# A decoder layer on one core: every engine's order rewritten without a loop, value products in one run, maxima transposed 128 columns wide, the context laid out transposed

## The chip, the core and the metric

The kernel runs on 1 of the 8 cores of a Trainium2 chip. A core has five engines, each with its own queue of instructions that it takes strictly in order: TensorE (PE, matrix products and transposes, with weight loads shown apart as PEld), VectorE (DVE), ScalarE (ACT), GpSimd (POOL) and SyncE (SP), which here issues all the transfers (DMAs). They are tied by semaphores alone. The metric is device time in microseconds (us), lower is better.

## What is computed

The reference is one decoder layer in float32 on 32 batches of 128 tokens by 128 features, with 16 heads of 8: self-attention with a bias by relative position, cross-attention on a context with a padding mask, and a feed-forward part whose activations are rounded to 8 bits and whose weights are ternary.

```
x = x + attn(LN(LN(x)))                  # softmax(q k / sqrt(8) + bias(i - j)) v, then w_out
x = x + xattn(LN(x), ctx, ctx, mask)     # the same with keys and values of ctx, masked scores
x = x + ffn(LN(x))                       # silu(gate) * up, then down; act_quant before each product
```

## The kernel before

All 32 batches stay in SBUF (`x_all`). Each batch goes through three stages, S (self-attention), X (cross-attention) and F (feed-forward), and one step of the program works on about nine batches at once, each at another place of the layer: `step(st)` of each engine calls its functions with `st.seq(lag)`, the batch that is `lag` steps behind. Lags are the table `FRONT_S, A_S, B_S, FRONT_X, A_X, B_X, POST_X, FFN2 = 0, 2, 3, 4, 5, 6, 7, 8`. Steps 0 to 9 and 30 to 39 are written out, steps 10 to 29 are five turns of a loop with four steps in it, in which semaphore values are worked out in registers.

What happens to one batch in an attention stage `a` (S or X):

- `normalise` (DVE) makes `xn`; TensorE transposes it (L1175, L1196), ACT copies it to `xnT`; `project_s` and `project_x` (L1210, L1224, L1225) give queries and keys, L1214 and L1192 the values, which ACT copies into `v_aug`.
- Queries and keys are split into three bf16 parts: `part1`, `part2` on ACT, `rest`, `part3` on POOL. SP writes them to HBM (`parts_out`, scratch, L288) and reads them back in another layout (`stack_in`, one transfer to `stack_q`, L306, and three to `stack_k`, L311).
- `scores_a` (L1059, four chunks `c` of four heads, banks 0 and 1) gives scores whose negated row maxima DVE takes (`row_max`, L826). POOL splits them into two bf16 parts of 16 columns (`neg_max_parts`, 32 columns), TensorE transposes them (`max_transposed`, L1154), ACT copies them (`maxT_out`), SP puts them into two rows of the stack (`max_in`, L327).
- `scores_b` (L1092, banks 2 and 3) gives the transposed scores less the maximum, ACT takes `exp` (L533) into `probs`, which S and X share, and `attend` (L1117, 4 products of 32 output rows each in a quarter of the array, for each of 4 chunks) multiplies with `v_aug`. In X a matrix product of 128x512 puts the mask into the bank first (L1055, L1088).
- `o_raw_out` (ACT), `o_transposed` (PE), `attend_sums` and `attend_norm` (DVE), `on_transposed`, `oT_out`, `project_out` (L1264), `residual` (DVE).

The context is loaded as it lies (`ctx_load`), transposed on TensorE (L1178) and copied by ACT (`ctxT_out`). The order of the work on each engine is the hand-written list of calls in its `step`. For TensorE it has, among others:

```
attend("X", st, post_x, 3)
scores_b("S", st, b_s, 0)
max_transposed("X", st, b_x)
...
attend("S", st, b_s, 0)
scores_b("S", st, b_s, 3)
attend("S", st, b_s, 1)
...
attend("S", st, b_s, 2)
project_out("X", st, post_x)
scores_a("S", st, a_s, 2)
attend("S", st, b_s, 3)
```

SP's `step` is `max_in X, ctx_load, stack_in S, store, parts_out X, max_in S, mask_load, parts_out S, stack_in X`. In the first four batches `keep_warm` puts four extra products ahead of the first `scores_b` of S.

Of the kernel before, what the change touches and what calls it, by code (L numbers as in the profile page):

```python
# [19 lines left out]
BF16 = mybir.dt.bfloat16  # L20
# [7 lines left out]
CH = 4  # L28
HC = H // CH
PARTS = 3  # L30
# [10 lines left out]
FRONT_S, A_S, B_S, FRONT_X, A_X, B_X, POST_X, FFN2 = 0, 2, 3, 4, 5, 6, 7, 8  # L41
CTX_T = 3
V_S = 1
LN_S = -1
DEPTH = 8
UNROLL = 4
LOOP_FROM, LOOP_TO = 10, 30
CONST_COLS = 8

ONES, POOL_CONST = 2, 15  # L50
# [4 lines left out]
WARM = 4  # L55
STACK_LOADS = 3 * len(REL_PAIRS) + 2


class Seq:


    def __init__(self, turn, base):
        self.turn, self.base, self.parity = turn, base, base % 2

    def count(self, per=1, upto=None):

        return self.turn * (UNROLL * per) + (self.base * per + (per if upto is None else upto))

    def parity_count(self, per=1):

        return self.turn * (UNROLL // 2 * per) + (self.base // 2 + 1) * per

    def at(self):

        return bass.ds(self.turn * UNROLL + self.base, 1)

    def before(self, n):

        in_loop = not isinstance(self.turn, int)
        return Seq(self.turn, self.base - n) if in_loop or self.base >= n else None  # L80


class Step:


    def __init__(self, turn, base):
        self.turn, self.base = turn, base

    def seq(self, lag):
        in_loop = not isinstance(self.turn, int)  # L90
        return Seq(self.turn, self.base - lag) if in_loop or 0 <= self.base - lag < B else None


def layer(nc, x, ctx, mask, w_self, w_cross, w_ffn, w_down, cols, w_out_s, w_out_x, bo_rows,
          rel_w, rel_const, scratch, scratch_rel, out):
    es = ExitStack()
    with es:
# [38 lines left out]
        ctx_in = sb("ctx_in", [S, 2, D])  # L136
# [6 lines left out]
        v_aug = {a: sb(f"v_aug_{a}", [S, 2, H // 2, 4, 16]) for a in "SX"}  # L143
# [16 lines left out]
        o_raw = sb("o_raw", [128, 2, S])  # L160
# [27 lines left out]
        def quarter(bank, n):  # L188
            return bank[:, n * 128:(n + 1) * 128]

        half_words = bank_s[:, 384:448]

# [3 lines left out]
            "mask_loaded0 mask_loaded1 ctx_loaded0 ctx_loaded1 pool_const dve_const pe_const stack_ready ctxT_ps "  # L196
            "ctxT_ready stats_S stats_X stats_F mv_S mv_X mv_F veps_S veps_X veps_F rstd_S rstd_X rstd_F xn_S "
            "xn_X xn_F shifted_S shifted_X xnT_ps_S xnT_ps_X xnT_S xnT_X qk_ps_S qk_ps_X v_ps_S v_ps_X q_S q_X "
# [14 lines left out]
        def value(eng, count):  # L213

            return count if isinstance(count, int) else eng.to_reg(count)

        def run(eng, step):

            for t in range(LOOP_FROM):
                step(Step(0, t))  # L220
            with eng.Fori(0, (LOOP_TO - LOOP_FROM) // UNROLL) as turn:
                for t in range(UNROLL):
                    step(Step(turn, LOOP_FROM + t))
            for t in range(LOOP_TO, B + DEPTH):
                step(Step(0, t))
# [5 lines left out]
        def _(sp):  # L231
# [43 lines left out]
            def parts_out(a, b):  # L275

                if not b:
                    return

                made = value(sp, b.count())
                free = b.before(2) and value(sp, b.before(2).parity_count(16 * (1 + PARTS)))
                sp.wait_ge(sems["dve_const"], REL_SPLIT)
                sp.wait_ge(sems["part3_" + a], made)
                if free:
                    sp.wait_ge(sems[f"stack_in_{a}{b.parity}"], free)
                sp.dma_start(scratch[a][b.parity].rearrange("o r t -> r o t"),  # L288
                             qk_parts[a][:].rearrange("r o n t -> r (o n) t"))\
                    .then_inc(sems["parts_out_" + a], 16)  # L290

            def stack_in(a, b):

                if not b:
                    return

# [1110 lines left out]
```

## Time and profile before

| what | value |
|---|---|
| median of 3 runs (lowest, highest) | 514.28 us (513.12, 520.25) |
| the profiled execution: span from first to last instruction | 513.4 us |
| PE, DVE, ACT, POOL busy | 454.1, 398.0, 372.9, 254.6 us |
| mean granted clock of TensorE | 0.967 |
| transfers | 62.48 MB, all of the program's own issued by SP |

The page gives no time around the profiled execution, so its span is set beside the median: 0.9 us less. A "step" in the text is the stretch between the starts of two following runs of value products of X (L1117 with `v_aug_X`) on TensorE. In a timeline of TensorE the ends of products are modelled and overlap; what an instruction costs there is the distance from its start to the start of the next.

### The profile page before, as it was taken

The page shows a single profiled execution, that of the slowest core. Times are in us where ns is not written, and L with a number is a line of the kernel's source. Part 1 is how long each engine was busy: PE and PEld are TensorE (multiplying, and loading weights), DVE is VectorE, ACT ScalarE, POOL GpSimd, SP SyncE. Part 2 cuts the span into 40 slices and gives each one's busy share as a digit, 9 for nine tenths or more (in the row PEclk, how much of TensorE's full clock was granted, in tenths as well). Part 3 has the DMA queues.
Part 4 walks back from the last instruction along what each step waited for, and adds up shares of the span by engine and source line. Part 5 has one row for each costly group of instructions (what it writes and reads, how often), then busy time and mean ns, then how long its engine had stood idle before and what let it go on. Part 6 is the DMA issues. An engine that isn't in the chain of part 4 may idle for free.

```text
span 513.4 us, 18365 instructions
## 1 busy us (share of the span) xinstructions
PE 454.1 (88%) x5596; PEld 328.0 (64%) x5596; DVE 398.0 (78%) x1154; ACT 372.9 (73%) x993; POOL 254.6 (50%) x691
## 2 busy tenths in 40 slices
PE   2246889999999999999999999999999999997762
PEld 1224556777777777777777777777777777764440
DVE  5722446799888889888888988889888888877553
ACT  0222556788888888888888888888888887775451
POOL 4221445655565555555566655555556654434110
PEclk9999789999999999999999999999999999999785
DMA  6264255555455545454445555544454555223000
GB/s 186 77 192 107 72 143 142 140 142 141 134 134 144 141 122 145 139 135 131 122 138 135 135 128 135 137 135 122 133 137 137 137 137 136 79 86 92 23 7 10
DMA packets 82191, 62.48 MB, mean 122 GB/s; under 512 B 57634, under 2 KB 71714, under 8 KB 82146
## 3 DMA queue, kind: packets, MB, share of 16 engines
q1 hardware_dynamic: 82146, 61.92, 44.4%
q8 instruction: 23, 0.38, 0.3%
q14 instruction: 22, 0.18, 0.1%
HBM read 46.47 MB, written 14.88 MB: 119 GB/s over the span
## 4 chain that ended last, share of the span: by engine, by line
PE 78%; DVE 5%; DMA 4%; issue 4%; SPq 3%; ACT 3%; POOL 1%; DVEq 0%; POOLq 0%; ACTq 0%
PE bank L1117 14%; PE bank L1092 12%; PE bank L1059 11%; PE bank L1088 6%; PE bank L1055 6%; PE bank L1264 4%; PE bank L1210 3%; PE bank L1138 2%; PE bank L1237 2%; PE bank L1175 2%; PE bank L1154 2%; PE bank L1295 2%; PE bank L1303 2%; PE bank L1224 2%; PE bank L1196 2%
## 5 line engine op out<-in xcount | busy, mean ns | idle before, releaser
L533 ACT ACTIVATE probs<-bank 128x512 f32<-128x512 f32 x256 | 145.5, 597 | 32.0 <-PE bank L1092 31.7
L826 DVE TENSOR_REDUCE neg_max_S<-bank 128x4 f32<-128x512 f32 x128 | 87.1, 685 | 34.3 <-PE bank L1059 34.2
L826 DVE TENSOR_REDUCE neg_max_X<-bank 128x4 f32<-128x512 f32 x128 | 84.2, 676 | 8.9 <-PE bank L1059 5.7
L1059 PE MATMUL bank<-stack_k_S,stack_q_S 120*128 120x128 bf16 x512 | 46.9, 227 | 12.9 <-DMA stack_k_S<-scratch_S 12.4
L432 POOL TENSOR_TENSOR qk_rest_X<-qk_X,qk_parts_X 128x256 f32<-128x256 f32 x32 | 21.4, 670 | 70.8 <-ACT qk_parts_X L536 70.8
L1092 PE MATMUL bank<-stack_q_S,stack_k_S 122*128 122x128 bf16 x512 | 52.5, 229 | 4.5 <-DMA stack_q_S<-neg_maxT_S 4.5
L1117 PE MATMUL bank<-probs,v_aug_S 128*32 128x128 f32 x1024 | 55.5, 291 | 0.0
L1055 PE MATMUL bank<-mask_bias,ident_bf 128*128 128x512 bf16 x128 | 49.4, 386 | 3.6 <-issue 2.3
L1092 PEld LDWEIGHTS bank<-stack_q_X,stack_k_X 74*128 74x128 bf16 x512 | 40.6, 99 | 16.4 <-issue 1.6
L1092 PE MATMUL bank<-stack_q_X,stack_k_X 74*128 74x128 bf16 x512 | 50.8, 222 | 0.0
L1088 PE MATMUL bank<-ident_bf,mask_bias 128*128 128x512 bf16 x128 | 50.3, 393 | 0.0
L1059 PE MATMUL bank<-stack_k_X,stack_q_X 72*128 72x128 bf16 x512 | 50.1, 220 | 0.0
L1059 PEld LDWEIGHTS bank<-stack_k_X,stack_q_X 72*128 72x128 bf16 x512 | 39.9, 98 | 16.0 <-issue 0.6
L1059 PEld LDWEIGHTS bank<-stack_k_S,stack_q_S 120*128 120x128 bf16 x512 | 36.8, 101 | 15.3 <-issue 14.0
L1092 PEld LDWEIGHTS bank<-stack_q_S,stack_k_S 122*128 122x128 bf16 x512 | 32.4, 101 | 21.2 <-issue 7.8
L855 DVE TENSOR_TENSOR x_all<-bank,x_all 128x128 f32 (+1 forms) x64 | 18.6, 291 | 25.7 <-PE bank L1264 24.3
L536 ACT ACTIVATE o_raw<-bank 128x256 f32<-128x256 f32 x64 | 24.8, 388 | 16.7 <-PE bank L1117 16.7
L1117 PE MATMUL bank<-probs,v_aug_X 128*32 128x128 f32 x1024 | 34.6, 276 | 0.0
L440 POOL TENSOR_TENSOR qk_parts_S<-qk_rest_S,qk_parts_S 128x256 bf16<-128x256 f32 x32 | 21.6, 675 | 21.0 <-ACT qk_parts_S L536 21.0
L609 ACT ACTIVATE hT<-bank,minus_round 128x512 bf16<-128x512 f16 x32 | 22.0, 686 | 12.4 <-PE bank L1295 12.4
L1117 PEld LDWEIGHTS bank<-probs,v_aug_S 128*32 128x32 f32 x1024 | 20.6, 109 | 14.8 <-issue 1.2
L1117 PEld LDWEIGHTS bank<-probs,v_aug_X 128*32 128x32 f32 x1024 | 26.0, 109 | 4.8 <-ACT probs L533 1.3
(159 smaller groups left out, 1159.1 us busy)
## 6 DMA issues: line engine op xcount, KB each, us to landing
stack_q_S<-scratch_S SPq DMA_DIRECT2D x32, 288.0 KB
stack_k_S<-scratch_S SPq DMA_DIRECT2D x96, 96.0 KB
stack_q_X<-scratch_X SPq DMA_DIRECT2D x32, 288.0 KB
stack_k_X<-scratch_X SPq DMA_DIRECT2D x96, 96.0 KB
scratch_S<-qk_parts_S SPq DMA_DIRECT2D x32, 192.0 KB, 2.3
scratch_X<-qk_parts_X SPq DMA_DIRECT2D x32, 192.0 KB, 2.3
ctx_in<-ctx SPq DMA_DIRECT2D x32, 64.0 KB, 2.7
mask_in<-mask SPq DMA_DIRECT2D x32, 64.0 KB, 1.8
```

Of the source, the lines that this page charges most:

```text
L432: pool.tensor_tensor(qk_rest[a][:], qk[a][:], qk_parts[a][:, :, 0, :], ALU.subtract)\
L440: pool.tensor_tensor(qk_parts[a][:, :, 2, :], qk_rest[a][:], qk_parts[a][:, :, 1, :], ALU.subtract).then_inc(sems["part3_" + a], 1)
L533: act.activation(probs[:, c, :], bank_b[c % 2][:, :], ACT.Exp).then_inc(sems["exp_" + a], 1)
L536: return act.activation(out_ap, in_ap, ACT.Copy)
L609: act.activation(hT[:].rearrange("p c s -> p (c s)"), bank_t[:, 0:256].bitcast(F16), ACT.Identity, bias=minus_round16[:, 0:1]).then_inc(se ...
L826: dve.tensor_reduce(neg_max[a][:, first_head(c):first_head(c) + 2 * HC - 1:2], bank_a[c % 2][:, :].rearrange("i (h j) -> i h j", h=HC), AX ...
L1055: pe.matmul(bank[:, :], ident_bf[:], mask_bias[:, p, :].unsqueeze(1).to_broadcast([S, HC, S]), start=True, stop=False)
L1059: last = pe.matmul(bank[:, part_of_bank(hh)], stack_q[a][rows, p, head(c, hh)], stack_k[a][rows, p, head(c, hh)], start=not masked, stop=n ...
L1088: pe.matmul(bank[:, :], mask_bias[:, p, :], ident_bf[:].unsqueeze(1).to_broadcast([S, HC, S]), start=True, stop=False)
L1092: last = pe.matmul(bank[:, part_of_bank(hh)], stack_k[a][rows, p, head(c, hh)], stack_q[a][rows, p, head(c, hh)], start=not masked, stop=n ...
L1117: last = pe.matmul(bank_o[32 * hh:32 * hh + 32, half * S:(half + 1) * S], v, probs[:, c, part_of_bank(hh)], start=u == 0, stop=u == 1, ski ...
L1264: pe.matmul(quarter(bank_s, 2), oT[a][:], w_o[a][:], start=True, stop=True)\
```

## The change

Each engine gets a new list of calls with new lags, and the loop is gone: all steps are written out, and each semaphore value is a constant. With it:

- `attend` of S runs as four chunks in a row, as that of X does; `probs` and `o_raw` are one each for S and X, `v_aug` has four copies for two.
- `neg_max_parts` is 128 columns wide (columns 32 to 127 zero), so its transpose is a full one.
- The host hands over the context transposed; it is loaded straight into `ctxT`, and transpose and copy are dropped.
- Queries, keys and values are projected together (`project_qkv`); the transposed `xn` of X goes to bank 4, and keys and queries are copied one by one.
- SP: `load_x(2)`, the 24 last batches of x, now comes ahead of the first `parts_out`; `stack_in` of S follows `parts_out` of S at once. DVE rounds the FFN weights (`ternary_weights`) after the first batch's maxima for before them.

Of the new `step` functions the diff shows three in part: first that of SP, then those of DVE and of TensorE. Their lags are counted from another step on each engine.

```
-LOOP_FROM, LOOP_TO = 10, 30
+STEPS = [(t, t) for t in range(-1, B + 14)]
+V_COPIES = 4
...
-        neg_max_parts = {a: sb(f"neg_max_parts_{a}", [S, M_ROWS, H], BF16) for a in "SX"}
+        neg_max_parts = {a: sb(f"neg_max_parts_{a}", [S, 128], BF16) for a in "SX"}
-        probs = sb("probs", [S, CH, HC * S])
+        probs = {a: sb(f"probs_{a}", [S, CH, HC * S]) for a in "SX"}
...
+            def step(st):
+                if st.of("S", 2) == 0:
+                    load_x(2)
+                mask_load(st, 10)
+                ctx_load(st, 8)
+                store(st, 14)
+                stack_in("X", st, 10)
+                max_in("X", st, 11)
+                parts_out("S", st, 6)
+                stack_in("S", st, 6)
+                parts_out("X", st, 9)
+                max_in("S", st, 7)
...
+            def step(st):
+                y_unit(st, 8)
+                ln_stats("S", st, -1)
+                attend_sums("S", st, 4)
+                y_inverse(st, 8)
+                attend_norm("S", st, 4)
+                quantise_y(st, 8)
+                row_max("X", st, 6, 1)
+                normalise("S", st, 0)
+                row_max("X", st, 6, 2)
+                row_max("X", st, 6, 3)
...
+            def step(st):
+                attend("S", st, 4, 0, ("xnT_X", 5), ("o_raw_X", 8), ("o_raw_S", 5))
+                attend("S", st, 4, 1)
+                attend("S", st, 4, 2)
+                attend("S", st, 4, 3)
+                scores_a("S", st, 3, 3, ("max_S", 3, 2), ("max_X", 7, 4), ("max_X", 7, 2), ("max_S", 4, 4))
...
-    named = {"x": a["x"], "ctx": a["ctx_1024"], "mask": a["mask_BxSxS2_ik0"], ...
+    named = {"x": a["x"], "ctx": a["ctx_1024"].transpose(0, 2, 1), "mask": a["mask_BxSxS2_ik0"], ...
```

**TensorE, one step, the value products of S (`probs`, `v_aug_S`), in the program before.** The numbers of the banks are kept; 32x128 is the shape of a product in a quarter of the array.

```order
L1117 MATMUL bank4<-probs,v_aug_S 32x128 x4
L1092 MATMUL bank3<-stack_q_S,stack_k_S 128x128 x4
L1117 MATMUL bank4<-probs,v_aug_S 32x128 x4
L1237 MATMUL bank6<-ident,o_norm_X 128x128
L1224 MATMUL bank7<-xnT_X,w_cross_sb 128x128
L1225 MATMUL bank7<-ctxT,w_cross_sb 128x128
L1117 MATMUL bank4<-probs,v_aug_S 32x128 x4
L1264 MATMUL bank6<-w_out_x_sb,oT_X 128x128
L1059 MATMUL bank0<-stack_k_S,stack_q_S 128x128 x4
L1117 MATMUL bank4<-probs,v_aug_S 32x128 x4
```

Now, with the products that end one step and begin the next:

```order
L1120 MATMUL bank6<-w_out_x_sb,oT_X 128x128
L1011 MATMUL bank0<-stack_k_S,stack_q_S 128x128 x4
L1047 MATMUL bank4<-probs_S,v_aug_S 32x128 x16
L1011 MATMUL bank1<-stack_k_S,stack_q_S 128x128 x4
L1143 MATMUL bank5<-ident_h,h_q 128x128 x4
L1079 MATMUL bank6<-ident,xn_S 128x128
```

Four groups of four, each between full-array products, have become one group of sixteen.

**SP, one full step, before** (`scratch` is HBM, written by `parts_out` and read by `stack_in`):

```order
L288 DMA scratch_S<-qk_parts_S 128x6x128 [waits s_stack_in_S1,s_part3_S,s_dve_const]
L306 DMA stack_q_X<-scratch_X 72x1x2048 [waits s_score_b_X,s_parts_out_X,s_dve_const]
L311 DMA stack_k_X<-scratch_X 24x1x2048 x3
L327 DMA stack_q_X<-neg_maxT_X 2x16x128 [waits s_score_b_X,s_maxT_X,s_dve_const]
L337 DMA ctx_in<-ctx 128x128 [waits s_ctxT_ps,s_dve_const]
L306 DMA stack_q_S<-scratch_S 72x1x2048 [waits s_score_b_S,s_parts_out_S,s_dve_const]
L311 DMA stack_k_S<-scratch_S 24x1x2048 x3
L356 DMA out<-x_all 128x128 [waits s_res_F,s_dve_const]
L288 DMA scratch_X<-qk_parts_X 128x6x128 [waits s_stack_in_X0,s_part3_X,s_dve_const]
L327 DMA stack_q_S<-neg_maxT_S 2x16x128 [waits s_score_b_S,s_maxT_S,s_dve_const]
L347 DMA mask_in<-mask 128x128 [waits s_mask_bias,s_dve_const]
```

Now:

```order
L276 DMA stack_q_X<-scratch_X 72x1x2048 [waits s_score_b_X,s_parts_out_X]
L281 DMA stack_k_X<-scratch_X 24x1x2048 x3
L293 DMA stack_q_X<-neg_maxT_X 2x16x128 [waits s_score_b_X,s_maxT_X]
L264 DMA scratch_S<-qk_parts_S 128x6x128 [waits s_stack_in_S1,s_part3_S]
L276 DMA stack_q_S<-scratch_S 72x1x2048 [waits s_score_b_S,s_parts_out_S]
L281 DMA stack_k_S<-scratch_S 24x1x2048 x3
L264 DMA scratch_X<-qk_parts_X 128x6x128 [waits s_stack_in_X0,s_part3_X]
L293 DMA stack_q_S<-neg_maxT_S 2x16x128 [waits s_score_b_S,s_maxT_S]
L310 DMA mask_in<-mask 128x128 [waits s_mask_bias]
L302 DMA ctxT<-ctx 128x128 [waits s_qkv_ps_X]
L317 DMA out<-x_all 128x128 [waits s_res_F]
```

The write of a batch's parts and the read that waits for it stood six transfers apart; now they stand next to each other, behind the stack of X.

**SP at the program's start, before**, behind the transfers of the bias:

```order
L288 DMA scratch_S<-qk_parts_S 128x6x128 [waits s_part3_S,s_dve_const]
L306 DMA stack_q_S<-scratch_S 72x1x2048 [waits s_parts_out_S,s_dve_const]
L311 DMA stack_k_S<-scratch_S 24x1x2048 x3
L288 DMA scratch_S<-qk_parts_S 128x6x128 [waits s_part3_S,s_dve_const]
L233 DMA x_all<-x 128x24x128
L337 DMA ctx_in<-ctx 128x128
```

Now:

```order
L215 DMA x_all<-x 128x24x128
L264 DMA scratch_S<-qk_parts_S 128x6x128 [waits s_part3_S]
L276 DMA stack_q_S<-scratch_S 72x1x2048 [waits s_parts_out_S]
L281 DMA stack_k_S<-scratch_S 24x1x2048 x3
L264 DMA scratch_S<-qk_parts_S 128x6x128 [waits s_part3_S]
L276 DMA stack_q_S<-scratch_S 72x1x2048 [waits s_parts_out_S]
```

The load of 24 batches has moved from behind the second batch's write to ahead of the first's.

## Rows read from the trace of the kernel before

**Rows 1.** The page: busy us (share of the span) and instructions of each engine.

```profile
PE 454.1 (88%) x5596; PEld 328.0 (64%) x5596; DVE 398.0 (78%) x1154; ACT 372.9 (73%) x993; POOL 254.6 (50%) x691
```

**Rows 2.** Windows: us, PE, PEld, DVE, ACT, POOL busy, clock, DMA share, GB/s.

```profile
115.66:128.68 13.02, 13.02 (x178) 9.78 (x176) 11.82 (x36) 11.43 (x32) 7.75 (x22) 1.00 0.53 140
...
195.67:249.22 53.55, 53.28 (x700) 39.23 (x697) 47.63 (x141) 46.26 (x125) 31.10 (x85) 1.00 0.49 133
```

**Rows 3.** Timeline of PE (start, us, what): value products of X, 25 steps apart.

```profile
103.38 1.08 PE L1117 MATMUL bank<-probs,v_aug_X 128*32 128x128 f32 x32
...
435.73 1.08 PE L1117 MATMUL bank<-probs,v_aug_X 128*32 128x128 f32 x32
```

**Rows 4.** Timeline of PE in a step outside the loop.

```profile
116.41 1.08 PE L1117 MATMUL bank<-probs,v_aug_X 128*32 128x128 f32 x32
117.42 0.40 PE L1092 MATMUL bank<-stack_q_S,stack_k_S 122*128 122x128 bf16 x4
117.75 0.23 PE L1154 MATMUL bank<-ident_bf,neg_max_parts_X 128*32 128x128 bf16 x1
117.91 0.40 PE L1092 MATMUL bank<-stack_q_S,stack_k_S 122*128 122x128 bf16 x4
118.14 0.39 PE L1138 MATMUL bank<-ident,o_raw 128*128 128x128 f32 x2
...
119.56 0.42 PE L1117 MATMUL bank<-probs,v_aug_S 128*32 128x128 f32 x8
119.92 0.40 PE L1092 MATMUL bank<-stack_q_S,stack_k_S 122*128 122x128 bf16 x4
...
122.83 0.27 PE L1178 MATMUL bank<-ident,ctx_in 128*128 128x128 f32 x1
122.94 0.39 PE L1295 MATMUL bank<-ident_h,h_q 128*128 128x128 f16 x4
```

**Rows 5.** Timeline of PEld: weight loads of 32 and of 128 columns.

```profile
221.13 0.09 PEld L1256 LDWEIGHTS bank<-ident_h,y_q 128*128 128x128 f16 x1
...
224.27 0.09 PEld L1154 LDWEIGHTS bank<-ident_bf,neg_max_parts_X 128*32 128x32 bf16 x1
```

**Rows 6.** Waits, 142.09 to 409.17 (the loop, 20 steps): us in total, times, longest.

```profile
DVE x_all L855 <- PE bank L1264: 10.3, 20, 0.6
...
DVE neg_max_S L826 <- PE bank L1059: 5.2, 20, 0.3
...
DVE xn_F L743 <- POOL rstd_F L416: 4.4, 20, 0.3
```

**Rows 7.** Lines of DVE in the loop: xcount, then busy us, mean ns, idle.

```profile
L743 DVE TENSOR_SCALAR xn_S<-x_all,mv_S,rstd_S 128x128 f32 x19 | 14.7, 774 | 0.0
...
L743 DVE TENSOR_SCALAR xn_X<-x_all,mv_X,rstd_X 128x128 f32 x19 | 6.6, 347 | 2.9 <-POOL rstd_X L416 2.3
```

**Rows 8.** Timeline of SP's queue; last, of all scratch_S transfers, issue to landing.

```profile
409.19 0.38 SPq L288 DMA_DIRECT2D scratch_S<-qk_parts_S  x1
409.67 0.80 SPq L306 DMA_DIRECT2D stack_q_X<-scratch_X  x1
410.52 2.10 SPq L311 DMA_DIRECT2D stack_k_X<-scratch_X  x3
412.73 0.68 SPq L327 DMA_DIRECT2D stack_q_X<-neg_maxT_X  x1
413.51 0.35 SPq L337 DMA_DIRECT2D ctx_in<-ctx  x1
...
DMA to landing us min/median/max: 2.3/2.3/7.4
```

**Rows 9.** The start: timelines of SP's queue and of PE.

```profile
30.40 5.66 SPq L337 DMA_DIRECT2D ctx_in<-ctx  x1
...
42.73 1.03 PE L1092 MATMUL bank<-stack_q_S,stack_k_S 122*128 122x128 bf16 x8 [4.50 <-DMA stack_q_S<-neg_maxT_S]
```

**Rows 10.** The chain that ended last, in order of time.

```profile
38.47 5.30 DMA stack_k_S<-scratch_S
```

More of the change, by code:

```diff
@@ L54, with __init__, of @@
 X_CUTS = (0, 2, 8, B)
-WARM = 4
+WARM, WARM_BATCHES = 4, 4
 STACK_LOADS = 3 * len(REL_PAIRS) + 2
[L59 to L80, printed above, removed]
-class Step:
[L86 to L91, printed above, removed]
+class Step:
+    def __init__(self, s, x):
+        self.first = {"S": s, "X": x, "F": x}
+    def of(self, stage, lag):
+        first = self.first[stage]
+        return first - lag if first is not None and 0 <= first - lag < B else None
+START = Step(0, None)
 def layer(nc, x, ctx, mask, w_self, w_cross, w_ffn, w_down, cols, w_out_s, w_out_x, bo_rows,
@@ L211, in first_head, with done, loaded, after @@
             return H // 2 * (c // 2) + c % 2
[L213 to L225, printed above, removed]
+        def done(b, per=1, upto=None):
+            return b * per + (per if upto is None else upto)
+        def loaded(b, per):
+            return (b // 2 + 1) * per
+        def after(eng, st, *users):
+            for name, lag, *signal in users:
+                stage = name[-1] if name[-2:] in ("_S", "_X") else "F"
+                b = st.of(stage, lag)
+                if b is not None:
+                    eng.wait_ge(sems[name], done(b, CH, signal[0]) if signal else done(b))
+                    return
+        def run(step):
+            for s, x in STEPS:
+                step(Step(s, x))
         block = es.enter_context(nc.Block())
@@ L273, in _, with parts_out @@
                         .then_inc(sems["stack_ready"], 16)
-            def parts_out(a, b):
-                if not b:
+            def parts_out(a, st, lag):
+                b = st.of(a, lag)
+                if b is None:
                     return
[L282 to L288, printed above, removed]
+                sp.wait_ge(sems["part3_" + a], done(b))
+                if b >= 2:
+                    sp.wait_ge(sems[f"stack_in_{a}{b % 2}"], loaded(b - 2, 16 * (1 + PARTS)))
+                sp.dma_start(scratch[a][b % 2].rearrange("o r t -> r o t"),
@@ L554, in xnT_out @@
[L554 to L566 removed]
+                act.wait_ge(sems["av_" + a], done(b, CH))
@@ L703, in _ @@
+                part2("X", st, 4)
+                o_raw_out("S", st, 3)
+                exp("X", st, 6, 0)
+                maxT_out("S", st, 2)
+                qk_out("S", 0, st, 0)
+                qk_out("S", 1, st, 0)
+                exp("X", st, 6, 1)
+                oT_out("S", st, 3)
+                part1("S", st, 0)
+                v_out("S", st, 0)
+                yT_out(st, 7)
+            run(step)
         @block.vector
@@ L1359 @@
+            run(step)
 _OUT = ((B, S, D), "float32")
```

1178 lines of the change are left out of this document (527 added, 651 removed).

## Prediction, made before the changed kernel ran

> **What bounds the kernel now.** I read the busy row of the page first: TensorE is busy for 454.1 us of a span of 513.4, 88%, with VectorE at 78% and ScalarE at 73% [rows 1]. A mean over the span can hide stages with other limits, so windows come next. In a full step outside the loop, TensorE is busy for all of the 13.02 us; VectorE has 11.82 and ScalarE 11.43. In a whole turn of the loop, four steps in 53.55 us, it is busy for 53.28 [rows 2]. So in the middle of the program a step lasts as long as TensorE's own list. Between the value products of X at 103.38 and those at 435.73 lie 25 steps, 13.29 us each [rows 3]. What lies before and behind them, 513.4 - 332.35 = 181 us, is fill and drain, in which steps are partly empty and the engines wait on latencies.
>
> A busy TensorE is not the same as one at its peak, so the price of each of its pieces is read from the distance between starts in its timeline [rows 4]. VectorE's waits are the third view: 19.9 us in the 20 steps of the loop in the three largest groups, 1.0 per step [rows 6]. VectorE's 47.63/4 = 11.9 and this 1.0 nearly fill a step, so it is next behind TensorE by little.
>
> **Part by part: TensorE.** Sixteen value products of X in one run take 117.42 - 116.41 = 1.01 us. A group of four of S takes .36 [rows 4]. Where a group of four begins behind full-array products, the four bf16 products ahead of it stretch too: such a group costs .33 (117.42 to 117.75) before a narrow operation and .23 (117.91 to 118.14) before a wide one. So changing into the narrow shape costs about .10, and the four groups of S cost 4 x (.36 + .10) = 1.84 us in a step. As one run they cost 1.01 + .10 = 1.11: **-.73**. The transposes of the maxima are narrow as well (32 output rows): .16 each plus .10 ahead. At 128 rows one is a plain bf16 product, a quarter of .23 = .06: 2 x (.26 - .06) = **-.40**. The transpose of the context took .11 [rows 4] and is gone: **-.11**. The sum is -1.24, and TensorE's list becomes 13.02 - 1.24 = 11.78 us. Every other product stays in number and shape; where it stands among float32 and bf16 neighbours changes, which I bound at .2 either way.
>
> The wider weights of the transpose are what speaks against it. The trace shows a load of 128 columns at .09 us and one of 32 columns at the same .09 [rows 5], so I charge nothing. By the Trainium skill, "TensorE: Matmul & The Clock Gate", section "LDWEIGHTS (loading the stationary operand)", load time grows with the columns at about one per clock of 1.2 GHz, 27 ns against 107; by that rule two transposes would give back .16 us per step, 4 us in all. The trace shows otherwise, and the measurement decides.
>
> **The loop.** A step of it took 53.55/4 = 13.39 us and one outside 13.02, .37 more, of which TensorE's gap is .07 and the rest slower pieces. Written out, all steps are of the second kind. That is within the 13.29 that I count from.
>
> **VectorE.** It keeps its instructions: 11.8 to 11.9 us a step. Its normalisation for S takes 774 ns on average where the same operation for X takes 347 [rows 7]; if its new neighbour on POOL lets it run at the price of X, .43 goes: 11.4 to 11.9. **ScalarE** had 11.43 and loses the copy of the context, to about 11.3. Neither can be left behind by a TensorE of 11.8 with slack to speak of: three engines then lie within half a microsecond.
>
> **SP.** Its issue costs per stage are .48 (parts_out, the distance to the next start), .85 and 2.2 (stack_in) and .78 (max_in), together 4.31; two stages and three single transfers at about .47 make 10.0 us a step [rows 8]. Behind parts_out of S, SP now waits for it to land before it issues the stack of S: at the median landing of 2.3 us [rows 8] that adds 2.3 - .48 = 1.8, 11.8 in all. Before, six transfers stood between the two and hid it. Queued behind SP meanwhile are parts_out of X and the maxima of S, for which TensorE waits in the end. The landing itself may be longer, since the write now follows the stack of X in the queues: a stack_k landed after 5.3 us at the start [rows 10], and the longest landing of the writes was 7.4 [rows 8]. I take 2.3, the median of the same transfer, and keep 5.3 for a rival.
>
> **The period.** Floors are 11.8 (TensorE), 11.4 to 11.9 (VectorE), 11.3 (ScalarE) and 11.8 (SP). Engines this close wait on each other now and then; before, TensorE's surplus of 1.1 us over VectorE absorbed that. I add .5 us, half of VectorE's present waits, since the new order moves every producer: **12.3 us**, with 11.8 as the lower end and 12.9 as the upper.
>
> **Fill and drain.** At the start SP stood 5.66 us at the context's transfer behind the load of 24 batches, and TensorE waited 4.50 us for the first maxima of S [rows 9]. With load_x(2) ahead of the first parts_out the stall moves to it, where it may cost the same; with the FFN weights rounded later, VectorE takes the first maxima earlier. Against it, POOL clears value buffers twice as large. From a gain of 6 (stall and wait mostly gone) to a loss of 2 (the memsets and a write held behind the large load), I take -3. The drain has shorter steps but is bound by latency: -1, bounds 0 and -3.
>
> **The sum.** 513.4 - 25 x (13.29 - 12.3) = 513.4 - 24.8 = 488.6; less 3 and 1 is 484.6. The median of the runs shown is 514.28, .9 above the profiled span, so **485.5 us**. The single largest term is the period: .1 us in it is 2.5 us in the time.
>
> **Rivals.** **A, the floors are reached.** TensorE was busy 100% of a step before, and if it is again, the period is 11.8: 513.4 - 25 x 1.49 = 476.1; with the better ends of fill and drain, near 6 and 1, it is 469.1, and 470 beside the median. For it: the full rows of TensorE [rows 2]. Against: SP and VectorE at the same floor.
>
> **B, the wait moves to VectorE.** It keeps its 1.0 us of waits on TensorE's products and POOL's results [rows 6], and 11.9 + 1.0 = 12.9 to 13.0 becomes the period: TensorE's shorter list only turns into idle time. Then 513.4 - 25 x .29 = 506.2, less 4, plus .9: 503. For it: the margin of VectorE was small, and its maxima are handed over one bank at a time. Against: part of the waits is there because TensorE was late, and goes when it is not.
>
> **C, slower: SP becomes the bound.** If the writes of S land after 5.3 us as the early stack did [rows 10], SP needs 10.0 + 5.3 - .48 = 14.8 us for its list, whatever the others do: 513.4 + 25 x 1.51 = 551.2, less 4, plus .9: 548. It decides from a landing of 3.8 us, at which SP's list is as long as the old step, and is a loss of 2% from about 4.4. For it: the write follows four transfers of the other stage's stack. Against: the median landing is 2.3, equal to the shortest.
>
> **D, the change does not do what it says**: if the price of the narrow groups is in fact the price of the exps that feed them, one run of sixteen waits for the last exp of S, and nothing is gained from the run; with the transposes alone (-.51) the period is 12.8 and the time 513.4 - 12.3 - 4 + .9 = 498. TensorE's busy share of 100% speaks against it.
>
> **Chances.** The forecast, 475 to 495: .58. A, below 475: .15. B and D, 495 to 505: .18. The rest: .05 for C and .04 for a time between 505 and 524 by a milder C. The 8-in-10 range takes in A's 470 and B's 503: 470 to 505. Two per cent is about what a measurement of this kernel can tell from no change, so the marks are 504 and 524.6: faster .88, within .07, slower .05.
>
> **What will show it.** In the new profile's windows of a middle step: a period near 12.3, TensorE busy 11.7 to 12.0 of it. In its timeline: value products of S as one run, 1.0 us to the next start; the transposes of the maxima with .06 behind them, and no stretched group ahead. In SP's timeline: the distance from parts_out of S to the stack of S, 2.3 us if I am right and 5 if C is. In VectorE's waits: under 1 us a step for me, as before or more for B. The prediction is wrong if the wide transposes cost more than the narrow ones, if a chain from the maxima through SP back to the scores is longer than its distance in the new lists, which no row of before can show, or if the longer fill of the new order eats what the steps give.

## The result, and the profile after

The changed kernel takes 541.36 us (median of 4 runs, 537.77 to 543.7) against 515.43 for the one before: 1.049 of its time, 95% interval 1.042 to 1.057. The forecast was 485.5 with a range up to 505. The profiled execution spans 537.8 us, 24.4 more than before.

The busy row of the page after answers to [rows 1]:

```profile
PE 413.7 (77%) x5533; PEld 326.1 (61%) x5564; DVE 413.7 (77%) x1154; ACT 360.0 (67%) x961; POOL 255.5 (48%) x693
```

TensorE has 40 us less to do, as the change intends, and no engine is above 77%. Where is the bound? The page's part on the chain that ended last, by engine and by line (its start):

```profile
DMA 40%; SPq 34%; PE 8%; issue 6%; DVE 6%; ACT 3%; POOL 2%; POOLq 0%; DVEq 0%; ACTq 0%
SPq L281 21%; DMA scratch_S<-qk_parts_S 19%; DMA scratch_X<-qk_parts_X 19%; SPq L276 9%; SPq L293 4%; PE bank L1011 1%; PE bank L1031 1%; PE bank L1028 1%; DMA stack_k_S<-scratch_S 1%; ACT h_q L617 1%; PE bank L1008 1%; DMA stack_q_S<-neg_m
```

74% of the way to the end lies in SP's queue (34%) and in transfers (40%, of which the two writes that SP stands behind are 38); L281 is `stack_k`, L276 `stack_q`. SP is not in the busy row at all, so the row alone hides it. The timeline of SP, one full cycle and the start of the next, answers to [rows 8]:

```profile
263.85 0.38 SPq L264 DMA_DIRECT2D scratch_S<-qk_parts_S  x1
266.94 0.80 SPq L276 DMA_DIRECT2D stack_q_S<-scratch_S  x1
267.80 2.02 SPq L281 DMA_DIRECT2D stack_k_S<-scratch_S  x3
269.93 0.38 SPq L264 DMA_DIRECT2D scratch_X<-qk_parts_X  x1
270.41 0.67 SPq L293 DMA_DIRECT2D stack_q_S<-neg_maxT_S  x1
271.13 0.44 SPq L310 DMA_DIRECT2D mask_in<-mask  x1
271.62 0.42 SPq L302 DMA_DIRECT2D ctxT<-ctx  x1
272.09 0.43 SPq L317 DMA_DIRECT2D out<-x_all  x1
274.05 0.80 SPq L276 DMA_DIRECT2D stack_q_X<-scratch_X  x1
274.89 2.36 SPq L281 DMA_DIRECT2D stack_k_X<-scratch_X  x3
277.36 0.68 SPq L293 DMA_DIRECT2D stack_q_X<-neg_maxT_X  x1
278.14 0.38 SPq L264 DMA_DIRECT2D scratch_S<-qk_parts_S  x1
```

There are two holes. From 264.23 to 266.94 SP stands 2.71 us between the write of S and the read of the same data; from 272.52 to 274.05 it stands 1.53 us before the read of X, though four issues lie behind that write. The cycle is 14.29 us: 10.05 of issues, as the prediction counted, and 4.24 of standing. The waits of SP from 100 to 400 us (us in total, times, longest) and the writes' landings of S, then of X, from 120 to 430 us say that it is so all along:

```profile
SPq L276 <- DMA scratch_S<-qk_parts_S: 62.9, 22, 3.8
SPq L276 <- DMA scratch_X<-qk_parts_X: 20.8, 19, 1.7
```

```profile
DMA to landing us min/median/max: 2.7/3.2/4.2
...
DMA to landing us min/median/max: 2.6/3.9/4.4
```

Both waits are for landings, not for an engine that feeds SP late. In the kernel before both writes landed after 2.3 us at the median; [rows 8] has that of S, the page's row and SP's timeline that of X:

```profile
scratch_X<-qk_parts_X SPq DMA_DIRECT2D x32, 192.0 KB, 2.3
```

```profile
308.78 2.03 SPq L311 DMA_DIRECT2D stack_k_S<-scratch_S  x3
...
313.78 0.39 SPq L288 DMA_DIRECT2D scratch_X<-qk_parts_X  x1
```

The write of X followed the stack of S there too, with one small transfer between, but in time it came 2.97 us behind the stack's last issue, since SP waited meanwhile for VectorE's result and for POOL's part3. Now it comes .1 us behind it, and the write of S .9 us behind the stack of X. The runs further down fall in line (median landing, distance in one step): 2.3 us at 2.5 (X in e7), 2.6 at 2.2 (S in e3), 3.0 at .8 (X in e3), 3.9 at .1 (X in e1). It is the time since the stack was issued that goes with the landing, not the place in the list alone.

The window over 22 steps (from the value products of X at 119.84 to those at 430.19; columns as in [rows 2]) gives a step of 310.35/22 = 14.11 us, with TensorE busy 12.0 and VectorE 12.4 of it:

```profile
119.84:430.19 310.35, 263.81 (x3785) 213.83 (x3806) 272.28 (x770) 243.65 (x661) 170.22 (x462) 0.99 0.49 130
```

By this cut the ends cost nothing. The value products of X of the first batch begin at 91.09 (before: 90.83), those of the last at 518.44 (494.44), and 19.4 us follow (19.0). All of the loss is in the 31 steps between. By the prediction's own cut, 25 steps from the second batch's value products of X to the 27th's, a step took (457.84 - 107.14)/25 = 14.03 us for 13.29, which is 18.4 of the 24.4 us; 3.8 came ahead of them and 2.3 behind.

### The profile page after: what moved, and what is told of

Its sections match the earlier page's. It is cut to its first block, busy times and chain, and to the rows that moved or that the text cites. A ratio compares the mean times of both kernels' runs of the same rounds, so it can differ in the third digit from the quotient of the medians.

```text
span 537.8 us, 17226 instructions
## 1 busy us (share of the span) xinstructions
PE 413.7 (77%) x5533; PEld 326.1 (61%) x5564; DVE 413.7 (77%) x1154; ACT 360.0 (67%) x961; POOL 255.5 (48%) x693
## 4 chain that ended last, share of the span: by engine, by line
DMA 40%; SPq 34%; PE 8%; issue 6%; DVE 6%; ACT 3%; POOL 2%; POOLq 0%; DVEq 0%; ACTq 0%
SPq L281 21%; DMA scratch_S<-qk_parts_S 19%; DMA scratch_X<-qk_parts_X 19%; SPq L276 9%; SPq L293 4%; PE bank L1011 1%; PE bank L1031 1%; PE bank L1028 1%; DMA stack_k_S<-scratch_S 1%; ACT h_q L617 1%; PE bank L1008 1%; DMA stack_q_S<-neg_maxT_S 1%; DVE neg_max_S L779 1%; PE bank L1143 1%; PE bank L1047 1%
## 5 line engine op out<-in xcount | busy, mean ns | idle before, releaser
L500 ACT ACTIVATE probs_S<-bank 128x512 f32<-128x512 f32 x128 | 75.0, 592 | 30.6 <-PE bank L1031 30.2
L500 ACT ACTIVATE probs_X<-bank 128x512 f32<-128x512 f32 x128 | 71.8, 590 | 25.7 <-PE bank L1031 25.5
L395 POOL TENSOR_TENSOR qk_rest_S<-qk_S,qk_parts_S 128x256 f32<-128x256 f32 x32 | 21.5, 672 | 101.0 <-ACT qk_parts_S L503 101.0
L1031 PE MATMUL bank<-stack_q_S,stack_k_S 122*128 122x128 bf16 x512 | 44.9, 228 | 29.8 <-DMA stack_q_S<-neg_maxT_S 29.2
L1011 PE MATMUL bank<-stack_k_S,stack_q_S 120*128 120x128 bf16 x512 | 46.9, 227 | 19.4 <-DMA stack_k_S<-scratch_S 17.1
L1011 PEld LDWEIGHTS bank<-stack_k_S,stack_q_S 120*128 120x128 bf16 x512 | 35.6, 101 | 27.5 <-issue 17.4
L1047 PE MATMUL bank<-probs_X,v_aug_X 128*32 128x128 f32 x1024 | 34.6, 276 | 0.0
L1047 PE MATMUL bank<-probs_S,v_aug_S 128*32 128x128 f32 x1024 | 34.6, 276 | 0.0
L1008 PEld LDWEIGHTS bank<-mask_bias,ident_bf 128*128 128x128 bf16 x128 | 12.7, 99 | 33.4 <-issue 17.5
L617 ACT ACTIVATE h_q<-h,round,h_scale 128x512 f16<-128x512 f32 x32 | 26.0, 813 | 7.1 <-DVE h_scale L906 7.0
L1047 PEld LDWEIGHTS bank<-probs_X,v_aug_X 128*32 128x32 f32 x1024 | 26.0, 109 | 4.8 <-ACT probs_X L500 1.3
L1047 PEld LDWEIGHTS bank<-probs_S,v_aug_S 128*32 128x32 f32 x1024 | 26.0, 109 | 3.3
```

Source lines behind the costliest of these rows:

```text
L395: pool.tensor_tensor(qk_rest[a][:], qk[a][:], qk_parts[a][:, :, 0, :], ALU.subtract)\
L500: act.activation(probs[a][:, c, :], bank_b[c % 2][:, :], ACT.Exp).then_inc(sems["exp_" + a], 1)
L617: act.activation(h_q[:], h[:], ACT.Identity, bias=round16[:, 0:1], scale=h_scale[:, 0:1])\
L1008: pe.matmul(bank[:, :], ident_bf[:], mask_bias[:, b % 2, :].unsqueeze(1).to_broadcast([S, HC, S]), start=True, stop=False)
L1011: last = pe.matmul(bank[:, part_of_bank(hh)], stack_q[a][rows, b % 2, head(c, hh)], stack_k[a][rows, b % 2, head(c, hh)], start=not masked ...
L1031: last = pe.matmul(bank[:, part_of_bank(hh)], stack_k[a][rows, b % 2, head(c, hh)], stack_q[a][rows, b % 2, head(c, hh)], start=not masked ...
```

## The experiments

Times are medians; the ratio is to the kernel before on the same chip, with its 95% interval. That kernel took 514.4 to 516.9 us there, so small differences between rows of different sets (e1 to e4, e5 to e8, e9 to e12) go by the ratios. The step is the mean of 20 to 22 middle ones.

The expectations speak of theories by name. SP: its queue, with its standing at both reads, sets the step. ORDER: SP only waits because the engines, in their new order, feed it late. TRANSFERS: the transfers themselves are late, whether or not SP stands at a read.

| kernel | us | ratio | step |
|---|---|---|---|
| before | 515.4 | 1 | 13.35 |
| changed | 541.4 | 1.049 (1.042 to 1.057) | 14.11 |
| e1: changed, write of S ahead of the stack of X | 624.0 | 1.208 (1.196 to 1.220) | 17.10 |
| e2: changed, read of S later | 581.3 | 1.127 (1.120 to 1.135) | 15.22 |
| e3: before, write and read adjacent | 544.6 | 1.056 (1.050 to 1.063) | 14.25 |
| e4: e1, load of x later | 625.2 | 1.210 (1.200 to 1.219) | 17.40 |
| e5: changed, no read behind a fresh write | 500.4 | .972 (.965 to .978) | 12.77 |
| e6: the same for S alone | 501.0 | .973 (.967 to .978) | 12.77 |
| e7: changed, front of S one batch ahead | 500.2 | .972 (.966 to .978) | 12.72 |
| e8: before, maxima 128 wide | 514.2 | .999 (.995 to 1.003) | 13.35 |
| e9: e7, POOL's rstd_X earlier | 492.1 | .955 (.950 to .959) | 12.39 |
| e10: e7, value products of S split | 529.2 | 1.026 (1.021 to 1.032) | 13.84 |
| e11: e7, maxima 32 wide | 501.8 | .971 (.968 to .974) | 12.75 |
| e12: e9, load of x later | 487.1 | .942 (.936 to .947) | 12.41 |

### e3: the adjacency alone, in the kernel before

```
                 ctx_load(st.seq(CTX_T - 1))
+                parts_out("S", st.seq(FRONT_S + 1))
                 stack_in("S", st.seq(FRONT_S + 1))
...
-                parts_out("S", st.seq(FRONT_S))
                 stack_in("X", st.seq(FRONT_X))
```

> The kernel before with parts_out of S moved from ahead of stack_in of X to right ahead of stack_in of S of the same batch: the adjacency of the changed kernel and nothing else of it. Theory SP: landing of 2.3 to 3.1 us less .48 at one read and .7 to 2.2 at the other on top of 10.0 us of issues is 12.5 to 14.9 a step, near 13.9 as in the changed kernel: 13.9 - 13.3 = .6 a step, about 530 (515 to 555). Rival ORDER: no change, 513 to 517.

544.6 us. One call moved in the old kernel costs 30 us (1.056), as much as the whole change does (1.049; the intervals overlap). ORDER expected no change here. The page has the same chain, 40% SP's queue and 34% transfers; and SP's waits in the loop are somewhat under those above, here with L302, the wait ahead of the read:

```profile
SPq L302 <- DMA scratch_S<-qk_parts_S: 41.7, 20, 2.6
SPq L302 <- DMA scratch_X<-qk_parts_X: 23.2, 19, 2.1
```

2.1 us a step at S and 1.2 at X. The adjacency alone is sufficient for a loss of this size; what the change does besides is not needed to explain it.

### e5 and e6: the same transfers, without the standing

```
-                sp.wait_ge(sems["parts_out_" + a], done(b, 16))
+                src = max(b - 1, 0) if a in "SX" else b
+                sp.wait_ge(sems["parts_out_" + a], done(src, 16))
...
-                parts = scratch[a][b % 2].rearrange("o (d h) t -> o d (h t)", d=HD)
+                parts = scratch[a][src % 3 if a in "SX" else src % 2].rearrange("o (d h) t -> o d (h t)", d=HD)
...
```

e6 has `a in "S"` in the same places. Neither is a kernel to use: the queries and keys that enter the scores are those of the batch before.

> The changed kernel in which each stack, of S and of X, is loaded with the parts of the batch before (scratch has three copies for two), so that every transfer is issued in the same order and with the same size, but no read stands behind a write that has just begun. The queries and keys of a batch are thus those of its predecessor; nothing else is left out. Theory SP: the list of SP is 10 to 11 us a step, the bound passes to VectorE (12.2 to 12.6) and the time is 541 - 27 x 1.5 = about 500 (490 to 508). Rival TRANSFERS (not the standing but the transfers themselves are late: contention among writes and reads of the stacks): above 525.

> The same for the stack of S alone; that of X still waits for the write of its own batch. Queries and keys of S are those of the batch before. Theory SP: 3.1 - .4 = 2.7 us of standing a step go and 1.2 to 1.6 of X stay, or grow by what S gave back: 11.2 to 12.5 a step, and a time within 5 us of the kernel without any standing. Rival TRANSFERS: above 525.

500.4 and 501.0 us: some 40 us less than the changed kernel, in the place that theory SP gave. All the bytes still move and every engine keeps its order, so neither the transfers nor the order of the engines holds the time up: rivals TRANSFERS and ORDER fall. And e6 shows that X's standing needs no cure of its own. With S's gone SP comes to X's write earlier, stands there for POOL's part3 instead (49.5 us in 22 steps), and the write of X lands in 2.3 us at the median again.

### e1, e2, e4: three ways to part them in SP's list alone

In e1, and in e4 together with the later load that e12 has below:

```
+                parts_out("S", st, 6)
                 stack_in("X", st, 10)
                 max_in("X", st, 11)
-                parts_out("S", st, 6)
                 stack_in("S", st, 6)
```

In e2:

```
                 parts_out("S", st, 6)
-                stack_in("S", st, 6)
                 parts_out("X", st, 9)
                 max_in("S", st, 7)
+                stack_in("S", st, 6)
```

> The changed kernel with one call moved: parts_out of S stands ahead of stack_in of X, as in the kernel before, so that the stack of X (3.7 us of issues) lies between the write and its read, and one more issue between the write of X and its read. Theory SP (its queue is the bound: it stands at both reads, 3.1 + 3.3 + 4.0 + 3.7 us a step): the list shrinks to about 10.3 us a step, the next floor is VectorE's 12.2 to 12.6, the step falls from 14.1 to about 12.6, and the time by 27 x 1.5 = 40 us to about 500. Rival ORDER (SP only waits because the new order of the engines feeds it late): the step stays near 14, and the time above 530.

> The changed kernel with stack_in of S moved behind parts_out of X and max_in of S instead: the write stays where the change put it, the read is 1.2 us of issues behind it, and 3.1 us more lie between the write of X and its read. Theory SP: about 1.5 us a step of waiting is left of 4.0, the list is some 11.5 us, below VectorE, but the stack of S lands 3 us later, which may show: 500 to 510. Rival ORDER: above 530, and worse than the changed kernel where the later stack is needed.

> The first of these kernels (parts_out of S ahead of stack_in of X) with the load of the 24 last batches six steps of SP later, behind the first two writes of S. In the changed kernel the first write took 7.9 us to issue behind that load and landed 11.6 us after its issue began. If that sets the fill, 5 to 8 us less than the first kernel; if the fill is set by later steps, or the load then holds up another transfer by as much, no difference beyond 2 us.

All three are far slower than the changed kernel. Theory SP missed the sign. ORDER's expectation fits e2 (above 530, worse than the changed kernel) and is far too low for e1 (a step near 14), but as an account of the changed kernel e3 and e5 rule it out. SP no longer stands at a read here; it waits for other engines instead: in e1 4.1 us a step for POOL's part3 of S and 3.0 for ScalarE's copy of the maxima of S. In e1, POOL's part3 of S (the parts that the write carries) stands behind `max_hi("X")` and `rstd_X` in POOL's new list. The stack of X now waits for it at the head of SP's queue, TensorE's scores of X wait for the stack, their maxima release `max_hi` again. Pieces of one turn in e1, of the chain and of SP's timeline:

```profile
266.88 0.56 POOL rstd_X L378
...
273.43 1.73 issue
275.15 0.38 PE bank L1008
```

```profile
268.08 0.38 SPq L264 DMA_DIRECT2D scratch_S<-qk_parts_S  x1
268.56 0.80 SPq L276 DMA_DIRECT2D stack_q_X<-scratch_X  x1
269.42 2.03 SPq L281 DMA_DIRECT2D stack_k_X<-scratch_X  x3
...
285.49 0.38 SPq L264 DMA_DIRECT2D scratch_S<-qk_parts_S  x1
```

A turn is 285.49 - 268.08 = 17.4 us. The chain names no releaser for TensorE's start at 275.15. That it is the stack of X is argued from SP: its last issue ends at 271.45, 3.7 us earlier, and the last transfer of the stack of S takes 3.7 to 4.0 us to land in e2. In e2 the stack of S is late instead: from 260 to 292 us the landing of its `stack_k_S` is 35.7% of the chain.

Part of the loss is TensorE's clock. Windows of e1, over 22 steps and behind the idle time that ends at 275.15:

```profile
128.61:504.91 376.30, 301.76 (x3785) 242.12 (x3806) 270.57 (x770) 243.26 (x661) 169.99 (x462) 0.90 0.39 106
...
275.92:279.30 3.38, 3.38 (x23) 3.04 (x22) 1.72 (x6) 0.67 (x2) 0.00 (x0) 0.51 0.57 144
```

The granted clock is given as a share of 2.4 GHz. TensorE had been without work for 2.9 us; from .8 us after its start it ran for 3.4 us at .51, the level of 1.2 GHz, where four bf16 products take .43 us for .23. The mean over the steps is .90 in e1, .89 in e4 and .95 in e2, against .99 in the changed kernel. As an estimate from these means, a fifth of e1's time is at the lower level and a tenth of e2's. If all of it lies on the way, that is about 1.6 of the 3.0 us by which a step of e1 is longer than the changed kernel's, and .6 of the 1.1 of e2.

So neither of the two orders tried parts the pair without making something else late: in these lists the first scores of S follow too closely on its last part. That no order of SP alone would do it is not shown.

### e7: the write one step ahead of the read

```
-STEPS = [(t, t) for t in range(-1, B + 14)]
+STEPS = [(t, t) for t in range(-2, B + 14)]
...
-                parts_out("S", st, 6)
-                stack_in("S", st, 6)
+                parts_out("S", st, 5)
+                if st.of("S", 5) == 0:
+                    stack_in("S", st, 5)
+                if st.of("S", 6) != 0:
+                    stack_in("S", st, 6)
...
-                rest("S", st, 3)
+                rest("S", st, 2)
...
-                project_qkv("S", st, 1, ("v_X", 5), ("h", 9), ("v_S", 2))
+                project_qkv("S", st, 0, ("v_X", 5), ("h", 9), ("v_S", 1))
```

and so on for every call ahead of the write of S on all engines. 

> The changed kernel with the whole front of S (statistics, normalisation, transposes, projections, parts, write) one batch further ahead on every engine, at unchanged places in the lists: SP writes the parts of one batch and reads those of the batch before, written a step ago. Everything of the reference is computed. Theory SP: the time of the kernel without standing of S plus what one more partial step of fill costs (3 to 12 us): 500 to 512, faster than the kernel before only if the first holds. Rival TRANSFERS or ORDER: above 525.

500.2 us, as e5, with the whole reference computed. The 3 to 12 us of longer fill in the expectation do not show: the value products of X begin at 86.35 us, for 91.09 in the changed kernel. The write and the read are neighbours in the list still, but of different batches, and SP passes at once:

```profile
254.25 0.38 SPq L264 DMA_DIRECT2D scratch_S<-qk_parts_S  x1
255.01 0.80 SPq L276 DMA_DIRECT2D stack_q_S<-scratch_S  x1
```

.76 us from issue to issue, for 3.09 in the changed kernel. The step is 267.10/21 = 12.72, of which TensorE is busy 12.1 and VectorE 12.1 (the window over 21 steps):

```profile
124.13:391.23 267.10, 255.00 (x3614) 205.41 (x3634) 254.34 (x732) 229.89 (x631) 161.66 (x439) 1.00 0.54 143
```

### e9: what is late next

e7's chain runs through three engines. Its pieces where it leaves TensorE:

```profile
250.67 0.70 DVE neg_max_X L782
...
252.84 0.56 POOL rstd_X L381
...
253.42 0.69 DVE xn_X L700
...
254.16 0.33 PE bank L1082
```

Three small products for the FFN (`h_units`) stand between the maxima and `rstd_X`, for which VectorE and then TensorE wait.

```
                 max_lo("X", st, 8)
-                h_units(st, 10)
                 variance("X", st, 6)
                 inverse_std("X", st, 6)
+                h_units(st, 10)
```

> The kernel with the front of S one batch ahead, and on POOL variance and inverse_std of X moved ahead of h_units. In that kernel's chain a step of 12.7 us runs through TensorE to neg_max_X, then POOL's neg_max_parts_X, three small h_units, rstd_X, DVE's xn_X (.69) and back to TensorE, which waits .4 a step there. Theory LOOP (that chain across three engines is the bound, not an engine's list): .57 us of h_units leave it, the step falls by .4 to .5 until VectorE's 12.1 takes over: 500 - 27 x .45 = about 488. Rival VECTORE (its list of 12.1 with stalls is the bound already): no change beyond 3 us.

492.1 us, step 12.39. The chain of its page is PE 70% (e7: 55%), and TensorE is busy 12.2 us of a step: its list is the next candidate, which no run here has tested. The edit does two things at once. Besides the .57 us of `h_units` that left POOL's way, VectorE's normalisation of X got faster, since POOL's part3 of S now begins .2 us behind it and not ahead of it. That is .33 us, and the step fell by .33. So e9 does not decide between LOOP (the way across three engines) and VECTORE (VectorE's own list, 12.1 us in e7 and 11.7 in e9): VECTORE had no gain only for a list that stays as long. For LOOP speaks the chain above. Groups of VectorE from 142 to 390 us in the changed kernel, in e7, then in e9 (for before, [rows 7]):

```profile
L697 DVE TENSOR_SCALAR xn_X<-x_all,mv_X,rstd_X 128x128 f32<-128x128 f32 x18 | 12.2, 677 | 0.2 <-POOL rstd_X L378 0.2
L895 DVE TENSOR_TENSOR down_scale<-h_step,mean_w 128x1 f32<-128x1 f32 x17 | 10.2, 600 | 0.0
...
L697 DVE TENSOR_SCALAR xn_S<-x_all,mv_S,rstd_S 128x128 f32<-128x128 f32 x18 | 6.1, 338 | 0.0
```

```profile
L700 DVE TENSOR_SCALAR xn_X<-x_all,mv_X,rstd_X 128x128 f32<-128x128 f32 x19 | 13.0, 683 | 0.0
```

```profile
L700 DVE TENSOR_SCALAR xn_X<-x_all,mv_X,rstd_X 128x128 f32<-128x128 f32 x20 | 7.1, 353 | 0.0
```

677 ns and 353 ns for the same operation. In the changed kernel it began at 260.35, beside POOL's part3 of S (260.28 to 260.95), and ended 261.04. The Trainium skill, "SBUF — State Buffer", section "Who interferes with whom", says that VectorE's operations that use both port pairs, as a tensor_scalar can, contend with GpSimd, and that whichever issues first holds the shared pair for its whole instruction while the other is fully blocked. The trace agrees in that VectorE's operation is the longer for POOL's, 677 against 353 ns, and 774 against 347 in [rows 7]. Two things it does not bear out. A block for the whole is not shown, since VectorE's ended .09 us after POOL's, less than the .35 that it needs alone. And POOL's part3 takes .67 us in both kernels, and so does its subtraction in the kernel before, where VectorE's operation began with it (273.64 and 273.67 us) and took .79.

### e8, e11, e10: the prediction's terms, one at a time

e8 widens the maxima's parts in the kernel before, e11 narrows them again in e7:

```
-                pe.transpose(half_words.bitcast(BF16), neg_max_parts[a][:], ident_bf[:])\
+                pe.transpose(half_words.bitcast(BF16)[0:M_ROWS * H, :],
+                             neg_max_parts[a][:, 0:M_ROWS * H], ident_bf[:])\
```

> The kernel before with nothing but the maxima's parts 128 columns wide (columns 32 to 127 zero), so that their transposes are full ones. By the prediction's term .40 us a step of TensorE goes, and TensorE is the bound of this kernel: 30 x .4 = 12 us less, 502 to 506. If VectorE, .1 to 1.1 us behind, takes over at once, 4 to 8 us less. If the narrow shape costs nothing (the stretch ahead of it is only how ends are modelled), 514.

> The kernel with the front of S one batch ahead, with the maxima's transposes 32 columns wide again. The term was .40 us a step of TensorE. In the kernel before it was worth nothing. Here, if TensorE is on the chain at both places: 27 x .4 = 11 us more, about 511; if the chain has other work there, no change.

Both make no difference: .999 (.995 to 1.003), and .971 beside .972 for e7. Yet TensorE's rows in e8 are just as forecast, .06 to the next start and .23 ahead, beside .16 and .33 in [rows 4]:

```profile
128.43 0.40 PE L1093 MATMUL bank<-stack_q_S,stack_k_S 122*128 122x128 bf16 x4
128.66 0.22 PE L1155 MATMUL bank<-ident_bf,neg_max_parts_X 128*128 128x128 bf16 x1
128.72 0.39 PE L1093 MATMUL bank<-stack_q_S,stack_k_S 122*128 122x128 bf16 x4
```

The rows have the price that was forecast, and it bought nothing. In the trace of the kernel before, the chain of the page is PE 78%; in e8 it is 59%, and it shows a second loop, at least as long as TensorE's list, that TensorE's full rows hid. It leaves TensorE behind `scores_a` of S and comes back at the transpose of y:

```profile
121.24 0.24 PE bank L1060 x4
...
122.71 0.58 POOL rstd_F L417
...
123.31 0.36 DVE xn_F L744
...
124.58 0.78 DVE xn_S L744
...
125.62 0.23 PE bank L1256
```

TensorE's busy time in the loop turn of [rows 2] went from 53.28 to 52.20 us, .27 a step for the .40 of the rows, and the turn did not get shorter: the step is 13.35 us in both kernels, idle time of TensorE taking the place of the work. The Trainium skill, "Perfetto Trace Analysis", section "Identifying the Most-Contended Engine", says that the busy share of TensorE's products is not a good measure of how close the kernel is to roofline. No run here measures that; what e8 shows is that the 100% of [rows 2] did not even make TensorE's list the bound.

e10 breaks up the run in e7 (edit against e7):

```
                 attend("S", st, 4, 0, ("xnT_X", 5), ("o_raw_X", 8), ("o_raw_S", 5))
-                attend("S", st, 4, 1)
-                attend("S", st, 4, 2)
-                attend("S", st, 4, 3)
                 scores_a("S", st, 3, 3, ...
+                attend("S", st, 4, 1)
                 h_transposed(st, 9, ...
+                attend("S", st, 4, 2)
                 xn_transposed("S", st, 0, ...
+                attend("S", st, 4, 3)
```

> The kernel with the front of S one batch ahead, with the value products of S again in four groups of four between full-array products (one group ahead, then behind scores_a, h_transposed and xn_transposed of S). By the prediction's term one run costs 1.11 us and four groups 1.84. If TensorE's list lies on the chain that sets the step: 27 x .73 = 20 us more, about 520. If the chain passes beside it, the slack of .6 a step swallows most: below 506.

529.2 us, a step of 13.84 for 12.72: 28 us by the ratios, more than the 20 expected. TensorE's timeline shows both parts of it:

```profile
260.45 0.43 PE L1050 MATMUL bank<-probs_S,v_aug_S 128*32 128x128 f32 x8
261.40 0.40 PE L1014 MATMUL bank<-stack_k_S,stack_q_S 120*128 120x128 bf16 x4 [0.52 <-DVE neg_max_S L782]
261.72 0.42 PE L1050 MATMUL bank<-probs_S,v_aug_S 128*32 128x128 f32 x8
262.08 0.40 PE L1146 MATMUL bank<-ident_h,h_q 128*128 128x128 f16 x4
```

A group takes .36 and the products ahead of it .32 for .22, the forecast's 1.84 for 1.11. The other .4 is a wait: three groups now stand behind a `scores_a` that waits .52 us for VectorE's maximum, where the whole run stood ahead of it and covered it. TensorE's idle time grew accordingly, from .58 to .99 us a step.

### e12: the load of the 24 batches

```
-                if st.of("S", 2) == 0:
+                if st.of("S", 8) == 0:
                     load_x(2)
```

> The first kernel of this set, with the load of the 24 last batches six steps of SP later. The prediction gave the start 3 us for the order of that load and the FFN weights. In the changed kernel the first write of S took 7.9 us to issue behind this load. If the first batch's way sets the fill, 4 to 8 us less than the first kernel of the set; if another transfer then takes the stall, within 2 us of it.

487.1 us against 492.1 for e9, a gain of 5.0. SP's first write of S in e9, then in e12:

```profile
20.16 8.23 SPq L264 DMA_DIRECT2D scratch_S<-qk_parts_S  x1
```

```profile
20.27 0.39 SPq L264 DMA_DIRECT2D scratch_S<-qk_parts_S  x1
```

The read of the first stack of S went from 32.08 to 25.13 us, and the first value products of X from 89.03 to 84.96.

In e4 the same edit gave nothing (625.2 beside 624.0, ratios 1.210 and 1.208).

## Why the prediction was wrong

**The step that failed is SP's sum**, "at the median landing of 2.3 us [rows 8] that adds 2.3 - .48 = 1.8, 11.8 in all". The 10.0 us of issues were right (10.05 measured). Two things were wrong in the rest. The landing was taken from rows in which the last stack had been issued some time before the write; it measured 3.2 us at .9 us behind the stack of X. And the second pair was not looked at: the change leaves four issues between the write of X and its read, as many as it needs at 2.3 us, but that write now follows the stack of S directly, landed after 3.9 us, and SP stood 1.5 us more in the cycle shown. With both, 10.05 + 2.7 + 1.5 is 14.3 in the cycle shown, and the mean step is 14.1. e3 shows that this alone makes a loss of the size measured, e5 to e7 that it goes with the standing. The prediction drew its chance for rival C, .05, from the first landing alone, and its threshold ("from a landing of 3.8 us") assumed one hole where there were two. C's mechanism is what happened, at two places and with a milder landing than the 5.3 us it was priced with: 541 for 548. That the number came so near is chance: a longer landing at one read stood in for two holes.

**The bound before** was read as TensorE alone, from a busy share of 100%. A second loop, across VectorE and POOL, was at least as long; e8 took work from TensorE and moved nothing. This is the second error, independent of the first. By itself it would have left the forecast inside its range: without the standing, the new lists give 12.72 to 12.77, where 12.3 was taken, and 500 us, not 485.5 (e5, e7). Rival B, "the wait moves to VectorE", with 12.9 and 503 us, came nearest to this in number; its mechanism was not tested by itself.

**TensorE's terms** were right by the distances between starts: 1.84 for 1.11 us (e10's rows), .26 for .06 a transpose (e8's); the whole list came to 12.0 us busy, for 11.8. The term of the context's transpose, -.11, was not tested. On the time they act as the chain lets them: the run of sixteen is worth 28 us in e7, a part of it a wait that it covers, the maxima nothing in either kernel.

**VectorE**: the .43 us of `xn_S` did go (774 to 338 ns), as the prediction allowed, but the new neighbours on POOL put .33 on `xn_X` (347 to 677) and .26 on `down_scale` (338 to 600). Its list was not 11.4 to 11.9 but 12.4 in the changed kernel, 12.1 in e7 and 246.44/21 = 11.7 in e9.

**Fill and drain**: -3 and -1 were forecast; by the prediction's own cut +3.8 and +2.3 were measured, with SP's standing in these steps too. The stall of 5.66 us [rows 9] moved to the first write, where it was 7.88 us long; e12 prices it at 5.0 us, in the kernel of e9.

**Left open**: which of the two reads has to be freed was tried for S alone (e6). X alone was not tried, nor a second issuing queue for the writes. In e1 the last link, the stack of X that TensorE waits for, was argued from landings. What holds the step of 12.39 in e9 was not tested, and why a landing takes longer soon after a stack is not shown.

## What to carry to other kernels

An issuing queue is an engine: add up its list over a step, its standing included, for every transfer whose source another transfer of the same queue has just written, and take the landing from a row where as much was issued ahead of it, as shortly before, as will be in the new order. Here such a pair was mended by setting it a whole batch apart, at unchanged places, while the two moves of one call only handed the wait to whatever was queued behind. And an engine that is busy 100% of a step need not be what sets it: take a little from it alone before you forecast by its list.

## What the runs showed of the hardware

The same write of 192 KB landed after 2.3 us at the median when the last of a stack of four had been issued 2.5 us or more before, after 3.2 us at .9 and after 3.9 at .1. A normalisation of 128x128 on VectorE took 338 to 353 ns alone and 677 to 774 ns where POOL's subtraction of 128x256 ran beside it, which took .67 us either way. An operation on a single column (`down_scale`) went from 338 to 600 ns with its new place, where it too has such a subtraction beside it (POOL from 265.17 to 265.84 us, `down_scale` from 265.25 to 265.85). A move of one call in SP's list changed the time by 30 to 83 us; in e1, the largest, TensorE's granted clock fell to the level of 1.2 GHz for 3.4 us behind 2.9 us without work.
